# Attention output kept in SBUF, projection and routing in one stage over pairs of batches, rank tables in 16 bits

## The reference

```python
# layer 1, after the heads: o is rounded by one scale for the whole tensor, then projected
o = fake_quant(o); h3 = h2 + o @ fake_quant(w_proj).T + b_proj
# switch: the router reads a normalised row, each expert takes 64 tokens of a sequence
normed = x * rsqrt(mean(x * x) + EPS) * ln_w
probs = softmax(normed @ w_router); expert = argmax(probs)
priority = cumsum(onehot(expert), axis=1); keep = priority <= 64
h = relu(expert_in @ wi[e]); out_e = h @ wo[e]
out = x + max(probs) * where(routed, out_e, normed)
```

## Time and profile before

| | |
|---|---|
| Median of 3 runs | 4544.15 us (4543.0 to 4547.32) |
| The profiled execution | own time 4545.12 us, span 4543.4 us |
| TensorE, VectorE | 3660.0 us (81%), 3453.7 us (76%) busy |
| ScalarE, GpSimd | 2567.5 us (57%), 1791.5 us (39%) busy |
| DMA | 478.49 MB, mean 105 GB/s |
| Granted clock | mean 0.811; 1.00 in 1200 to 2300 us, 0.50 in 2630 to 4049, 0.98 in 4049 to 4543 |

### The profile page before, as it was taken

The page is one execution under the profiler, slowest core; times in us unless marked ns, Lnnn a source line. Parts: engine busy times, 40 slices in busy tenths (PEclk is TensorE's granted clock), DMA queues, the critical chain, the costliest instruction groups (busy, mean ns, idle before and its releaser), DMA issues. The chain is left out here.

```text
span 4543.4 us, 72547 instructions
## 1 busy us (share of the span) xinstructions
PE 3660.0 (81%) x23492; PEld 2809.3 (62%) x23540; DVE 3453.7 (76%) x6522; ACT 2567.5 (57%) x5065; POOL 1791.5 (39%) x2216
## 2 busy tenths in 40 slices
PE   0069999998599999999996768888688853559999
PEld 0059999997499999999995411111122223459999
DVE  7948888887677778777767589999777755855565
ACT  4645555553344444444444689999788842434433
POOL 5757777776233334334330022222100012434444
PEclk9999999999799999999995655555555555569999
DMA  4334554554322222221224770010122245434432
GB/s 115 98 104 139 142 142 129 147 139 124 79 83 89 89 89 89 89 73 68 79 86 132 247 281 24 24 31 17 60 72 72 72 131 159 131 116 125 129 113 86
DMA packets 293421, 478.49 MB, mean 105 GB/s; under 512 B 47690, under 2 KB 226010, under 8 KB 282206
## 3 DMA queue, kind: packets, MB, share of 16 engines
q1 hardware_dynamic: 271646, 448.77, 31.9%
q0 software_dynamic: 20480, 25.87, 1.9%
q10 hardware_dynamic: 1024, 0.54, 0.0%
HBM read 347.60 MB, written 136.51 MB: 107 GB/s over the span
## 5 line engine op out<-in xcount | busy, mean ns | idle before, releaser
L1101 POOL TENSOR_TENSOR c_ap<-c_ac,c_ap 128x420 fp32r<-128x420 f32 x340 | 428.1, 1259 | 743.6 <-ACT c_ap L1260 743.1
L726 PE MATMUL b_pA<-ab_woutT,b_ys 128*105 128x192 f32 x3840 | 689.4, 326 | 1.2 <-ACT b_ho L646 0.4
L726 PEld LDWEIGHTS b_pA<-ab_woutT,b_ys 128*105 128x105 f32 x3840 | 610.6, 171 | 12.1 <-ACT b_ho L646 3.9
L564 POOL TENSOR_TENSOR b_ys<-b_hs,b_cb 128x525 f32<-128x525 f32 x384 | 506.5, 1319 | 222.4 <-DVE b_hs L791 180.3
L1985 DVE TENSOR_REDUCE g_raw<-g_pS 128x1 f32<-128x525 f32 x816 | 549.6, 703 | 31.4 <-PE g_pS L1940 30.2
L1961 ACT ACTIVATE g_pS<-g_pS,g_stt 128x525 f32<-128x525 f32 x816 | 553.6, 777 | 19.8 <-POOL g_stt L1914 19.0
L1940 PE MATMUL g_pS<-g_qk 16*128 16x262 bf16 (+1 forms) x1536 | 461.2, 408 | 94.5 <-ACT g_pS L1961 36.0
L1260 ACT ACTIVATE c_ap<-c_ac 128x420 fp32r<-128x420 f32 x340 | 189.3, 557 | 571.2 <-DVE c_ac L1427 569.5
L791 DVE TENSOR_TENSOR_SCAN b_hs<-b_ae,b_pB 128x525 f32<-128x525 f32 x384 | 479.4, 1248 | 41.2 <-ACT b_ae L665 7.3
L1169 PE MATMUL c_pD<-cw_wd,c_ap 128*105 128x192 f32 x4080 | 438.2, 257 | 27.3 <-POOL c_ap L1101 27.3
L1169 PEld LDWEIGHTS c_pD<-cw_wd,c_ap 128*105 128x105 f32 x4080 | 423.6, 171 | 51.4 <-POOL c_ap L1101 39.0
(11 more groups left out here) (387 smaller groups left out, 8155.5 us busy)
## 6 DMA issues: line engine op xcount, KB each, us to landing
b_cb<-dram_ct SPq DMA_DIRECT2D x64, 1050.0 KB, 5.9
c_wb<-dram_wt SPq DMA_DIRECT2D x60, 840.0 KB, 9.7
b_cb<-dram_ct SPq DMA_DIRECT2D x64, 525.0 KB
dram_slots<-g_empty SPq DMA_DIRECT2D x32, 772.0 KB
c_wb<-dram_wt SPq DMA_DIRECT2D x20, 1050.0 KB, 6.4
o_xr<-dram_slots SPq DMA_DIRECT2D x64, 258.0 KB, 4.6
dram_qk<-f_qk SPq DMA_DIRECT2D x16, 787.5 KB
g_qk<-dram_qk SPq DMA_DIRECT2D x16, 787.5 KB, 4.5
```

The lines of the kernel that those rows point to most:

```text
L564: pool.tensor_tensor(ys[:, u % RING, :], hs[:, u % RING, :], cb[:, g % 3, u % GU, :], ALU.mult).then_inc(s["ys"], 1)
L726: ins = pe.matmul(into, ys[:, u % RING, t * TP:(t + 1) * TP], woutT[:, u % NU, :], start=(u == 0 and t % 2 == 0), stop=(u % NU == NU - 1), ...
L1101: nc.gpsimd.tensor_tensor(ap[LO][:, r, :], ac[:, r, :], ap[HI][:, r, :].bitcast(F32), ALU.subtract)\
```

## The change

1. The heads write their output into one SBUF tensor `O` of all 16 batches, which lives until the routing is done. The store of `o` and its load are gone.
2. The projection's block is gone. Its work stands in the routing's block, which now takes two batches (ten tiles) at once, all written out, no loop. `h3` is not stored; `base` holds `h2` from the load, then bias and projection are added in place, and the result of the tokens is written over it too. `O` is rounded in place.
3. The product with the layer's weights is done in place in `nx`, which has two buffers of a pair in place of four of a batch. `pY` holds one batch.
4. The split of the first expert's weights moves from the routing's end to the front of the experts' block, since their tiles (`wi_s`, `wi_t`, `wo_s`) are allocated there now.
5. `tri`, `c1` and `c2` of `dense_experts` are BF16.

```diff
-        tri = sb("tri", [TP, E, E])
+        tri = sb("tri", [TP, E, E], BF16)
-        c1, c2 = sb("c1", [TP, CT, E, E]), sb("c2", [TP, CT, E, E])
+        c1, c2 = sb("c1", [TP, CT, E, E], BF16), sb("c2", [TP, CT, E, E], BF16)
...
-                sp.dma_start(scratch["o"][b], oT[:, k, :, :].rearrange("p g l -> p (g l)")).then_inc(s_o[k], 16)
...
-                v.tensor_copy(oT[:, k, g, 0:QM], pO[:, :]).then_inc(s["ev"], 1)
+                v.tensor_copy(O[:, b, g, 0:QM], pO[:, :]).then_inc(s["ev"], 1)
...
+            pool.wait_ge(s_w, 48)
+            biased(0)
+            pool.iota(tok[:, :], pattern=[[TP, NT]], base=0, channel_multiplier=1).then_inc(s_tok, 1)
...
+            for m in range(NP):
+                if m + 2 < NP:
+                    biased(m + 2)
+                pool.wait_ge(s["prob"], at(m, 1, 1))
+                pool.wait_ge(s["bas"], at(m, 1, 1))
+                for j in range(TW):
+                    pool.indirect_dma_start(slots, bass.IndirectOffsetOnAxis(ap=to[:, m % 2, j:j + 1], axis=0),
...
+            def project(b):
+                pe.wait_ge(s["oq"], at(b, 1, 1))
+                pe.wait_ge(s["y"], at(b, 1, 0))
+                for t in range(TT):
+                    for g in range(HG):
+                        ins = pe.matmul(pY[:, t // 2, t % 2 * D:(t % 2 + 1) * D], oq[:, b % 2, g, t * TP:(t + 1) * TP],
+                                        K["wpT"][:, g, :], start=(g == 0), stop=(g == HG - 1))
+                ins.then_inc(s["Y"], 1)
...
+            project(0)
+            project(1)
+            for q in range(2):
+                transposes(0, q)
+            logits(0)
+            project(2)
+            for m in range(NP):
+                if m + 1 < NP:
+                    project(2 * m + 3)
+                places(m)
+                if m + 1 < NP:
+                    for q in range(2):
+                        transposes(m + 1, q)
+                    logits(m + 1)
+                if m + 2 < NP:
+                    project(2 * m + 4)
...
+            for b in range(4):
+                rounded(b)
+            rows(0)
+            bases(0)
+            for q in range(2):
+                copies(0, q)
+            for m in range(NP):
+                if m + 2 < NP:
+                    for q in range(2):
+                        rounded(2 * m + 4 + q)
+                if m + 1 < NP:
+                    rows(m + 1)
+                act.wait_ge(s["lg"], at(m, 1, 1))
+                nc.scalar.activation(ex[:, :, :], lg[:, :, :], ACT.Exp).then_inc(s["ex"], 1)
+                if m + 1 < NP:
+                    bases(m + 1)
+                    for q in range(2):
+                        copies(m + 1, q)
...
+            for m in range(NP):
+                st = Steps(dve, s_ro, VR, m)
+                if m + 1 < NP:
+                    statistics(m + 1)
+                choice(m, st)
+                if m + 1 < NP:
+                    normed(m + 1)
+                destinations(m, st)
+                shares(m)
+                outputs(m)
+                if m + 2 < NP:
+                    for q in range(2):
+                        integers(2 * m + 4 + q)
+                st.end()
```

More of the change, by code:

```diff
@@ L2325, in _ @@
             st.after(v.tensor_tensor(K["co"][:, 2:3], K["sc"][:, 7:8], K["sc"][:, 2:3], ALU.mult))
[L2328 to L2420, removed]
-            integers(0, 0, 0)
-            def body(b, i, k, last):
-                if last < 2:
-                    integers(b + 1, i + k, 1 - k)
-                dve.wait_ge(s["Y"], at(b, 1, 1))
-                dve.wait_ge(s["hb"], at(b, 1, 1))
-                dve.wait_ge(s_o[k], i * 16)
-                for c in range(3):
-                    n = 2 if c < 2 else 1
-                    ins = v.scalar_tensor_tensor(y[:, k, 2 * c:2 * c + n, :],
-                                                 pY[:, k, c, 0:n * D].rearrange("p (t d) -> p t d", t=n),
-                                                 K["co"][0:TP, 2:3], hb[:, k, 2 * c:2 * c + n, :], ALU.mult, ALU.add)
-                ins.then_inc(s["y"], 1)
-            two_a_turn(dve, NB, body)
@@ new lines, in destinations @@
+            def destinations(m, st):
+                dve.wait_ge(s["cum"], at(m, 1, 1))
+                st.after(v.tensor_tensor(pr[:, :, :], pC[:, :, :], oh[:, :, :], ALU.mult))
+                st.after(v.tensor_reduce(place[:, :], pr[:, :, :], AX, ALU.add))
+                st.counted(v.tensor_scalar(over[:, :], place[:, :], float(CAP), 1.0e6, ALU.is_gt, ALU.mult))
+                st.after(v.tensor_tensor(slot[:, :], slot[:, :], place[:, :], ALU.add))
+                dve.wait_ge(s_sc[m % 2], m // 2 * (16 * TW))
+                v.tensor_tensor(to[:, m % 2, :], slot[:, :], over[:, :], ALU.add).then_inc(s["dest"], 1)
+                dve.wait_ge(s["dest"], at(m, 1, 1))
@@ new lines, in shares, with outputs @@
+            def shares(m):
+                dve.wait_ge(s["ex"], at(m, 1, 1))
+                v.tensor_reduce(sums[:, :], ex[:, :, :], AX, ALU.add).then_inc(s_go, 1)
+                dve.wait_ge(s_go, 2 * m + 1)
+                v.reciprocal(prob[:, :], sums[:, :]).then_inc(s_go, 1)
+                dve.wait_ge(s_go, 2 * m + 2)
+                v.tensor_copy(nx[:, m % 2, :, 2 * D], prob[:, :]).then_inc(s["prob"], 1)
+            def outputs(m):
+                dve.wait_ge(s["bas"], at(m, 1, 1))
+                for j in range(TW):
+                    ins = v.scalar_tensor_tensor(base[:, m % R, j, :], nx[:, m % 2, j, 0:D], prob[:, j:j + 1],
+                                                 nx[:, m % 2, j, D:2 * D], ALU.mult, ALU.add)
+                ins.then_inc(s["ou"], 1)
@@ new lines, in _ @@
+            integers(0)
+            integers(1)
+            statistics(0)
+            integers(2)
+            integers(3)
+            dve.wait_ge(s_tok, 2)
+            v.tensor_copy(first_f[:, :], first_i[:, :, :].rearrange("p b t -> p (b t)")).then_inc(s_f, 1)
+            dve.wait_ge(s_f, 1)
+            dve.wait_ge(s_i, 2)
+            normed(0)
+            for m in range(NP):
+                st = Steps(dve, s_ro, VR, m)
[8 more added lines that the diff above has]
+                if m + 2 < NP:
+                    for q in range(2):
+                        integers(2 * m + 4 + q)
+                st.end()
```

861 lines of the change are left out of this document (408 added, 453 removed).

## The result

The changed kernel takes 4505.65 us (median of 4 runs, 4503.24 to 4515.72) against 4544.81 for the kernel before on the same chip: a ratio of 0.9915, 95% interval 0.99 to 0.9931. Forecast were 4509 and 4480 to 4530. The profiled execution, the fastest of the four, has a span of 4501.5 us, 41.9 less than the one of before; between the medians it is 39.2.

A forecast was written before the change was run, and what follows sets the result against it. Transfers set the projection's pace; in the joined stage a one-pair circle through three engines binds. -29.5 for joining, +0.8 experts' start, -6.6 tables make -35.3: 4509.8 from the profiled execution, median 1.0 lower, 4509 us; range 4480 to 4530.

The forecast's parts named there:

- The circle: Joined stage: one pair in flight, rows to next rows through TensorE, VectorE and ScalarE, 35.3 us per pair, seven times.
- Idle VectorE: Joined stage: VectorE idles about 9 us per pair in front of the result of `project(2m+2)`.
- Head and tail: Joined stage: first load 3689.9 to first rows written 3729.3; after seven circles, 3976.4 to the experts' first load 4020.3.
- The 7.5: Tail: 7.5 us taken from last scatter to experts' first load; if all of 11.9 is needed, -25.1 instead of -29.5.
- The 0.8 us for the heads' last store: Head: without the last store of `o`, the stage's first DMA was taken at 3689.9 instead of 3690.7.
- The experts' start: Front of experts' block: moved weight split delays first `hidden` to some 7.9 us behind first load, from 7.2: +0.8.
- The tables: Dense experts: 16-bit rank tables save 6.6 us, between -20 and +16; rival that they give more, 4480 to 4495, chance 0.05.
- The gap of 0.98: Dense experts: TensorE's 0.98 us wait for `c_ac` behind L1351, forecast to fall to 0.7.
- The clock: Joined stage: forecast to stay at 0.50; rival that TensorE's clock rises, 4465 throughout or 4486 if late, chance 0.14.
- The scatters: Joined stage rival: ten scatters over 22 us instead of 12.7 make rows wait for landing, slower, 4550 to 4570; chance 0.05.
- the -29.5: Joined stage against the two old ones: experts' first load at 4020.3 instead of 4049.8, 29.5 us saved.
- the 27.4: Later forecast for both projections ahead of the logits: period of L2538 falls from 34.46 to about 27.4 us, time about 4457.

The follow-up runs named there:

- the fastest kernel: Changed kernel with both projections ahead of the logits, bias on VectorE, small loads first and GpSimd's constants not waiting for them: 4443.24 us, ratio 0.9772.
- the reordered kernel: Changed kernel with one edit in TensorE's order, both next projections placed ahead of the logits: 4469.97 us, ratio 0.9831.

## Why the prediction was right, step by step

- **The circle** came out as 34.46 us where the sum gave 35.3, and link for link: first transposes, first copies, second transposes and second copies end at 4.2, 5.7, 7.8 and 9.0 behind the rows (forecast 4.3, 6.1, 8.1, 9.4), logits at 16.3 (16.8), projection at 18.8 (19.4), both results at 24.6 (25.2), chain at 29.9 (30.7), rows at 34.5. Of the 0.8 too much, 0.3 is in the first copies, which start at 4.6 and not at 4.9, 0.1 in the logits (7.25 for 40 where two groups of 20 were 3.69 each), the rest in handovers and the chain. Times seven it is 5.9 of the 6.6 us by which the profiled execution beat the sum (41.9 against 35.3). That TensorE's order binds is shown: the projections ahead of the logits take 36 us off (4505.65 to 4469.97), and 3.3 us more VectorE work in the cover leaves the period at 34.46.
- **Idle VectorE**, forecast as about 9 us a pair: 9.71.
- **Head and tail.** 40.2 us from the first load to the written rows (39.4 forecast), 43.8 from there to the experts' first load (43.9). In the head the 1.7 us assumed for iotas and masks were 2.6; no row ahead of the prediction shows them. That the tail came out to 0.1 us is luck, as its two parts were off in opposite ways: the last scatter ends 34.2 behind the rows, not 36.4, and 9.6 us pass behind it, not 7.5. By the trace this scatter lands 1.9 us behind its end, and 7.7 pass from there. The 7.5 had stood behind `low_parts`, beside which the landing could lie. The 9.6 is inside the 7.5 to 11.9 that the prediction named. The 0.8 us for the heads' last store can't be told: from the last store of the dense stage to this stage's first load it is 1291.9 us before, 1291.8 after, and up to 1295.5 in the other runs.
- **The experts' start**: +0.9 against +0.8, up to the first hidden matmul. From the first load to the end of the kernel it is 493.3 us against 493.5 before, so this 0.9 is lost in the scatter of that stretch. Nothing of expert 1's load is seen in TensorE's waits.
- **The tables**: -6.3 in the profiled execution, -5.1 in the mean, against -6.6; so the profiled one looks 1.2 us better than it should. The gap of 0.98 is 0.72 (0.7 forecast). L1351 shows 1.08 where it showed 1.21: it still ends right behind GpSimd's step beside it. The big ones fell from 1.22 to 0.69, and the reduction (L1355) stayed at 1.22 on 1024 elements. The Trainium skill's tier table ("VectorE: DVE Perf Modes") says both, twice the rate for the first and none of it for the second; the trace agrees.
- **The rivals.** The clock stayed at 0.50 in the stage, through 10 us of logits and projection back to back seven times over. The Trainium skill's "TensorE: Matmul & The Clock Gate" (Part 1) would have had activity release it; by this trace such stretches don't. Why it did rise for 7 us in the fastest kernel stays open, so the rival was worth its chance. The scatters take 0.96 plus 0.30, with one of 2.8 us in most pairs; ten take 12.4 to 15.6, below the 22 from which they would bind.
- **What the prediction didn't ask** is which part of the -29.5 is owed to what. It set a joined stage against two old ones. The runs divide it: taking `O`'s round trip through DRAM out of the projection, with its loops written out, is worth 54 us by itself (359.15 to 305.05, and 52.6 by the medians), in line with transfers as its pace, which the prediction's first part said. Writing the two stages as one then gives back 19 to 24: 18.9 and 22.3 by the medians, 20.2 and 23.5 by the stages in the traces. Separate stages take 3.5 us for a batch's projection and 12.3 for its routing, 31.6 a pair; the circle of the joined one takes 34.5. With the projections ahead of the logits and the bias on VectorE it takes 26.8, and then the joining pays: 4453.59 us against the 4486.75 of the two stages, on the same chip.
- Where a later sum failed: the 27.4 for the reordered kernel had no term for GpSimd's bias beside the chain (4 us, five times), though the head of the prediction had counted such a collision as 1.0.

## What to carry to other kernels

Two stages in one are not faster by being one. Add up the circle from one step of an item to the same step of the next item, and compare it with the sum of the two old periods, not with the engines' busy time. Here it was 34.5 against 31.6 us as written, and 26.8 once the order was right. If an engine's queue has a long piece whose result is needed late (the logits) ahead of a short one that is needed at once (the projection), turn them round before anything else; here that was worth 36 us, and 52 once a collision was out of the way too. And cost the parts of a change apart: the gain here was one part's, and another part was hiding a loss of 20 us behind it.

## What the runs showed of the hardware that I had not expected

VectorE is held by GpSimd's elementwise work only in some of its steps. A tensor_scalar on ten elements took 4.15 us beside a bias of 4.22, and a scalar_tensor_tensor on twenty (L79) 4.17; the pair of tensor_scalar steps of L2589 that takes 1.87 alone took 5.90 beside a bias in the changed kernel's head. The scalar_tensor_tensor of the result (L2598) and bn_stats (L2603) beside the same bias kept their 1.47 and 1.40. So it is not the kind of operation alone: L2598 reads one operand from PSUM (`pY`), L79 reads both from SBUF. This was read from the traces, not tried out one operation at a time, and what separates the steps stays open.

In the two kernels with `O` in SBUF and separate stages the granted clock rose for part of the projection (0.57 and 0.68 in the mean of the stretch). The matmuls of a batch took down to 1.44 us there, 2.64 at 0.50:

```profile
3746.14 1.44 PE L2388 MATMUL i_pY<-k_wpT,i_oq 128*105 128x192 bf16 x15 [1.10 <-DVE i_oq L2402]
```

The stretch took 69.7 and 67.6 us, with TensorE busy for 39.0 and 34.0 of it: TensorE was not its pace. So the clock rose in a stage in which TensorE did batches of 2.6 us with gaps of 0.3 to 2.1 us ahead of the rises, and did not in the changed kernel's stage with stretches of 10 us. Why is open.
